# Graph-network layer: SyncE fetches the rows of four whole groups, six a step, where it fetched two groups and the last, four a step

## The reference, cut to what matters

```python
h = jnp.maximum(_layernorm(x, axis=-1), 0.0)
p1 = jnp.tanh(h @ pp_W1 + pp_b1) @ pp_W2 + pp_b2
inter = jnp.concatenate([p1[src], p1[dst]], axis=-1)
inter = (inter @ pi_W1 + pi_b1) @ pi_W2 + pi_b2
inter = (inter @ pi_W3).reshape(E, 64, 8)
i1 = jnp.einsum('ecb,eb->ec', inter, edge_attr)
i1 = jnp.tanh(i1 @ ii_W1 + ii_b1) @ ii_W2 + ii_b2
return x + jax.ops.segment_sum(i1, dst, num_segments=6250)
```

## Time and profile before

| | |
|---|---|
| Median of 3 runs | 1979.13 us (1978.99 to 1981.69) |
| The profiled execution | 1983.09 us, its span 1981.2 us |
| TensorE busy | 1733.1 us (87%) |
| VectorE busy | 1449.0 us (73%) |
| ScalarE busy | 1109.5 us (56%) |
| POOL busy | 1479.1 us (75%) |
| Mean granted TensorE clock | 0.96 of full speed |

### The profile page before, as it was taken

One profiled execution on the slowest core, in us unless ns is written; L12 is line 12 of the kernel. 1 busy time (PEld: TensorE's weight loads), 2 busy tenths in 40 slices (PEclk: granted clock), 3 DMA queues, 4 the chain that ended last, 5 costly groups with the idle time before them and its releaser, 6 DMA issues.

```text
span 1981.2 us, 58993 instructions
## 1 busy us (share of the span) xinstructions
PE 1733.1 (87%) x20012; PEld 1134.5 (57%) x20012; DVE 1449.0 (73%) x1939; ACT 1109.5 (56%) x2419; POOL 1479.1 (75%) x1569
## 2 busy tenths in 40 slices
PE   7699999989988898888888888888888888888998
PEld 6466566655555555555555555555555555555666
DVE  7688778877677777677777777677777767777766
ACT  5666656655555555555555555555555555555554
POOL 7777777777777777777777777777777777777773
PEclk9799999999899999999999999899999999999999
DMA  6543333333333332332333323333233233332331
GB/s 141 115 82 62 67 67 64 61 65 66 58 63 58 62 66 56 63 62 56 62 55 61 62 56 60 61 63 64 55 63 62 56 59 62 59 59 54 59 71 44
DMA packets 266170, 127.83 MB, mean 65 GB/s; under 512 B 188169, under 2 KB 238328, under 8 KB 265864
## 3 DMA queue, kind: packets, MB, share of 16 engines
q1 hardware_dynamic: 214767, 74.86, 17.9%
q0 software_dynamic: 49664, 50.96, 15.4%
q10 hardware_dynamic: 1558, 0.15, 0.1%
HBM read 119.42 MB, written 6.00 MB: 63 GB/s over the span
## 4 chain that ended last, share of the span: by engine, by line
POOL 62%; issue 21%; PE 11%; ACT 2%; DMA 1%; SPq 1%; DVE 1%; ACTq 0%; DVEq 0%; POOLq 0%
POOL u_rows L568 62%; PE bank L1379 5%; PE bank L1474 1%; PE bank L1362 1%; DMA loc_bc<-loc_tab 1%; PE bank L1386 1%; PE spread_ps L1371 1%; DVE o_sb L987 1%; PE bank L1346 1%; ACT st_sb L756 0%; SPq L472 0%; SPq L440 0%; PE spread_ps L1208 0%; PE bank L1356 0%; DMA v_tab<-acc_all 0%
## 5 line engine op out<-in xcount | busy, mean ns | idle before, releaser
L568 POOL DMA_INDIRECT u_rows<-u_tab,src_e x1424 | 1352.4, 950 | 434.1 <-issue 433.1
L987 DVE TENSOR_TENSOR o_sb<-st_sb,spread_ps 128x2048 f32<-128x2048 f32 x391 | 892.9, 2284 | 365.0 <-PE spread_ps L1371 346.8
L756 ACT ACTIVATE st_sb<-bank,s_bias 64x256 f32<-64x256 f32 x1564 | 734.3, 469 | 438.0 <-PE bank L1362 406.9
L1379 PE MATMUL bank<-o_sb,g_sb 128*64 128x256 f32 x6256 | 807.0, 403 | 1.0 <-DVE o_sb L987 0.8
L1379 PEld LDWEIGHTS bank<-o_sb,g_sb 128*64 128x64 f32 x6256 | 433.5, 143 | 232.9 <-issue 36.7
L1362 PE MATMUL bank<-ident,u_rows 128*128 128x128 f32 x1436 | 259.3, 304 | 191.9 <-DMA u_rows<-u_tab,src_e 191.0
L1051 DVE TENSOR_TENSOR hot_t<-loc_bc,bank 126x512 bf16<-126x512 bf16 x391 | 268.8, 688 | 144.0 <-PE bank L1474 59.7
L1362 PEld LDWEIGHTS bank<-ident,u_rows 128*128 128x128 f32 x1436 | 189.8, 192 | 240.5 <-DMA u_rows<-u_tab,src_e 228.0
L1474 PEld LDWEIGHTS bank<-hot,t_sb 128*65 128x65 f32 x3128 | 216.1, 139 | 158.6 <-issue 150.6
L744 ACT ACTIVATE tt_sb<-bank,z_bias 128x256 f32<-128x256 f32 x391 | 185.4, 474 | 175.1 <-PE bank L1379 174.4
L1474 PE MATMUL bank<-hot,t_sb 128*65 128x42 f32 x3128 | 262.8, 235 | 9.1 <-DVE acc_all L1100 8.6
(11 more groups left out here) (148 smaller groups left out, 353.3 us busy)
## 6 DMA issues: line engine op xcount, KB each, us to landing
loc_bc<-loc_tab SPq DMA_DIRECT2D x391, 126.0 KB
u_rows<-u_tab,src_e POOLq DMA_INDIRECT x1424
sp_stage<-u_tab SPq DMA_DIRECT2D x1344, 0.2 KB
v_win<-v_tab SPq DMA_DIRECT2D x391, 15.8 KB
basis<-edge_attr SPq DMA_DIRECT2D x24, 256.0 KB, 4.2
v_tab<-acc_all SPq DMA_DIRECT2D x6, 336.0 KB
basis<-u_tab,src_e POOLq DMA_INDIRECT x100, 2.7
u_tab<-basis SPq DMA_DIRECT2D x6, 224.0 KB
```

The source lines that it names most:

```text
L568: pool.indirect_dma_start(out=u_rows[:, g % UR, j, :] if g >= AHEAD else first_u[:, g - XG, j, :], out_offset=None, in_=u_tab[:, :], in_of ...
L756: last = nc.scalar.activation(tiles[h * D:(h + 1) * D, j], s_ps[part].rearrange("p (q a e) -> p q a e", q=2, a=TILES), ACT.Identity, bias= ...
L987: return nc.vector.tensor_tensor(o_sb[:, r, :, :].rearrange("p c (j e) -> p j c e", j=TILES), st_sb[:, r, :].rearrange("p (j e) -> p j e", ...
L1379: last = nc.tensor.matmul(z_ps[h * D:(h + 1) * D, 0:2 * P], g_sb[:, c, :], o_sb[:, r, c, 2 * h * P:(2 * h + 2) * P], start=(c == 0), stop= ...
```

## The change

SP fetches four whole groups, 96, 183, 270 and 357, and no longer the last one. A fetch takes `ROWS = 6` rows a step, so 86 steps (the last with 2 rows): steps 4 to 89, 91 to 176, 178 to 263 and 265 to 350, 344 fetching steps and 2048 rows. The row numbers lie in one partition of `sp_idx` and are loaded `AT_ONCE = 8` at a time whenever the row's number is a multiple of eight, so three steps of four have one load and the fourth has none: 64 loads a group, 256 in all. The staged group goes to `u_rows` in one DMA of 1 KB a partition in the place of four of 256 bytes. POOL gathers 380 groups where it gathered 381, with group 390 last, for which it also waits for the last input load. The passes of TensorE that stand written out move with the skipped groups.

```diff
-    BY_SP = [(135, 4, P), (263, 132, P), (NG - 1, 260, PART)]
+    ROWS = 6
+    BY_SP = [(96, 4), (183, 91), (270, 178), (357, 265)]
+    AT_ONCE = 8
...
-        sp_idx = sb("sp_idx", [P, len(BY_SP) * TILES], i32)
+        sp_idx = sb("sp_idx", [1, len(BY_SP) * GE], i32)
...
             def load_sp_idx():
-                for k, (g, _, n) in enumerate(BY_SP):
-                    sp.dma_start(sp_idx[0:n, k * TILES:(k + 1) * TILES],
-                                 src[g * GE:g * GE + n * TILES].rearrange("(p j) -> p j", j=TILES)
+                for k, (g, _) in enumerate(BY_SP):
+                    sp.dma_start(sp_idx[0:1, k * GE:(k + 1) * GE], row(src[g * GE:(g + 1) * GE])
                                  ).then_inc(sp_idx_in, 16)
 
-            def fetch_rows(k, p):
-
-                _, at = nc.values_load_multi_w_load_instructions(
-                    sp_idx[p:p + 1, k * TILES:(k + 1) * TILES], engines=[mybir.EngineType.SP], min_val=0, max_val=N - 1,
-                    skip_runtime_bounds_check_because="src names nodes of x")
-                for j in range(TILES):
-                    sp.dma_start(sp_stage[p:p + 1, k % 2, j, :], u_tab[bass.ds(at[j], 1), :]
+            def fetch_rows(k, rows, at):
+
+                for r in rows:
+                    p, j = divmod(r, TILES)
+                    if r % AT_ONCE == 0:
+                        _, at = nc.values_load_multi_w_load_instructions(
+                            sp_idx[0:1, k * GE + r:k * GE + r + AT_ONCE], engines=[mybir.EngineType.SP], min_val=0,
+                            max_val=N - 1, skip_runtime_bounds_check_because="src names nodes of x")
+                    sp.dma_start(sp_stage[p:p + 1, k % 2, j, :], u_tab[bass.ds(at[r % AT_ONCE], 1), :]
                                  ).then_inc(sp_rows_in[k], 16)
+                return at
 
             def place_fetched(k):
 
-                g, _, n = BY_SP[k]
-                sp.wait_ge(sp_rows_in[k], 16 * TILES * n)
-                for j in range(TILES):
-                    sp.dma_start(u_rows[:, g % UR, j, :], sp_stage[:, k % 2, j, :]).then_inc(fetched[k], 16)
+                g, _ = BY_SP[k]
+                sp.wait_ge(sp_rows_in[k], 16 * GE)
+                sp.dma_start(u_rows[:, g % UR, :, :], sp_stage[:, k % 2, :, :]).then_inc(fetched[k], 16)
...
-                    for k, (of, first_at, n) in enumerate(BY_SP):
+                    for k, (of, first_at) in enumerate(BY_SP):
                         if k >= 2 and g == first_at:
                             sp.wait_ge(s_ready, BY_SP[k - 2][0] + 1)
-                        if 0 <= g - first_at < n:
-                            fetch_rows(k, g - first_at)
+                        if first_at <= g:
+                            at = fetch_rows(k, range(ROWS * (g - first_at), min(ROWS * (g - first_at + 1), GE)), at)
...
                 for g in range(XG, NG):
                     k = g // PIECE
+                    if g == FULL:
+                        pool.wait_ge(last_in, 32)
...
-                for of in skipped[:-1]:
+                for of in [of for of in skipped if of < LOOP_END]:
```

More of the change, by code:

```diff
@@ L469, in _ @@
                 load_sp_idx()
+                at = None
                 for g in range(NG):
@@ L560, in _ @@
                     k = g // PIECE
+                    if g == FULL:
+                        pool.wait_ge(last_in, 32)
                     if g % PIECE == 0:
                         pool.wait_ge(ld[k % LD], ld_count(k))
-                    if g in [of for of, _, _ in BY_SP]:
+                    if g in [of for of, _ in BY_SP]:
                         continue
@@ L1409, in y_late @@
                     last.then_inc(y_ps, 1)
-            skipped = [of for of, _, _ in BY_SP]
+            skipped = [of for of, _ in BY_SP]
             def step(n, u, first, last_pass, g=None, fetched_pass=False, gone=(0,) * UN):
@@ L1436, in newest @@
                         if fetched_pass and n + u in skipped:
-                            pe.wait_ge(fetched[skipped.index(n + u)], 16 * TILES)
+                            pe.wait_ge(fetched[skipped.index(n + u)], 16)
                         else:
@@ L1504, in _ @@
                     at += UN
-                with pe.Fori(at, LOOP_END, UN) as n:
-                    for u in range(UN):
-                        step(n, u, False, False, gone=gone)
+                if at < LOOP_END:
+                    with pe.Fori(at, LOOP_END, UN) as n:
+                        for u in range(UN):
+                            step(n, u, False, False, gone=gone)
                 for n in range(LOOP_END, NG + 5, UN):
@@ L1510, in _ @@
                         step(n, u, False, True, fetched_pass=True, gone=gone)
+                        if n + u in skipped:
+                            gone[u] += 1
                 pe.wait_ge(acc_done, NG)
```

## The result

The changed kernel takes 2028.6 us (median of 4, 2026.52 to 2029.3) where the kernel before took 1980.41 beside it: ratio 1.0241, 95% interval 1.0223 to 1.0259. It is 2.4% slower, some 48 us. The side was forecast, the size was not: 1987 us was forecast, with 2000 as the upper end.

What follows compares the result with a forecast made beforehand. SP was taken to bound up to step 350 (1449.7 + 264.6 - 76.5 + 1.8 = 1639.6 us for 330 steps), then TensorE; +8 us on the median 1979.13 gave 1987 us, range 1968 to 2000.

Steps and rivals of the forecast that it cites:

- who would bind: Up to step 350 SP, at 4.97 us a step, sets the pace instead of POOL; from there TensorE does.
- the two ends: Before and behind SP's 330 steps: `loc_bc` of step 20 at 154.6 us; from step 350 at 1794.2 to span end 1988.4.
- the price of a row: On SP, steps 20 to 349: 630 more row fetches at 0.42 us each, +264.6 us.
- rows get dearer in bursts of six: Rival, sharing 10% with TensorE losing clock: row fetches cost more six in a row, giving 2000 us or more.
- Loads: SP's register loads, steps 20 to 349: 244 instead of 330, 86 fewer at 0.89 us, -76.5 us.
- I take the same price for both: SP's register load of eight numbers costs the same as one of four, 0.89 us with its gap.
- The sign named for it: In the profile after, SP's `loc_bc` of step 84 at about 473 us, its step 4.97 us from there to 350.
- the 7.2 of the forecast's sum: Whole span: 1988.4 us forecast against 1981.2 in the profile before, +7.2 us, made +8 for work at step 352.
- the range: 1968 to 2000 us for the whole kernel; the forecast case's own range, SP as the bound, was 1983 to 1998.
- a rule: Rival at 1%: SP's load is priced by the register, some 200 ns each, +0.8 us x 256, about 2190 us.
- POOL's wait: POOL, held by its ring, waits some 10 us in all, most of it before 250 us, in place of 0.9.

Runs made afterwards that it cites:

- The trim of SP's register instructions: The changed kernel without the runtime bounds checks on the window starts: 1983.54 us, ratio 1.0015 to the kernel before the change.

## Why the prediction was wrong

**Right: who would bind.** "Nothing hides this. SP's slack was used to catch up": POOL's share of the chain went from 62% to nothing, TensorE no longer waits for gathered rows, VectorE waits for `loc_bc` until step 350. The trim of SP's register instructions shows it: 45 of the 48 us came back with nothing else changed.

**Right: the two ends.** `loc_bc` of step 20 was forecast at 154.6 and came at 153.87. From `loc_bc` of step 350 to the end of the span 1988.4 - 1794.2 = 194.2 us were forecast and 2026.3 - 1830.43 = 195.9 measured; TensorE did run at 4.45 us a step there with L1400 (L1394 before).

**Right: the price of a row.** 0.42 us was taken for a further row; that is what the records average, in bursts of six too. The rival "rows get dearer in bursts of six" gave the nearest time, 2000 or more, and names the wrong cause: its time came out by luck.

**Wrong: the term "Loads", -76.5 us.** It is the step "I take the same price for both". The rows it rested on, 783 ns for eight window starts and 814 for four row numbers, differ in two things: the window starts are loaded behind row fetches (42 of the 49 loads), the row numbers behind `v_win` (312 of 336). The one costs four numbers more, the other the place, 0.23 and 0.25 us, and they cancelled in the comparison. In place of -76.5 the traces show, for steps 20 to 349: 80 loads behind `v_win` at 1.08, 4 behind an input load at 0.81 and 160 between rows at 0.83, so 223 us, against 330 at the 0.845 that a load took in the saturated stretch before, 279 us: -56. To it comes the second half of the same mistake: 243 steps now have no load ahead of their first row, which takes 0.54 where 0.47 was paid behind a load before: +16. The sum is about -40 and not -76.5, and 36 us is what SP's step was off: (5.08 - 4.97) x 330 = 36.3. The sign named for it, `loc_bc` of step 84 at about 473, came at 479.8. In the spans, 2026.3 - 1981.2 = 45.1 us are these 36, the 7.2 of the forecast's sum and 1.7 behind step 350. The other 3 of the 48 are the place of the two profiled executions among their runs: the one before took 2.7 us more than its median, the one after 0.5 less.

**Wrong: the range.** I wrote that 0.01 us on a row is 19.5 us, and bounded the row. The load I let go only down to 0.81, which bounds it on the side of the rows that I had already compared wrongly. Had each of the 244 loads been given 0.2 us more as an upper end, 49 us, the range would have reached 2036. On the strength of that comparison I had put it down that eight numbers cost no more than four; they cost 0.057 us a number (medians of 560, 787 and 1238 ns for four, eight and sixteen). On it I had also put a rule aside: the Trainium skill, Runtime: NRT & Kernel Launch (Instruction fetch mechanics), gives a TENSOR_LOAD as some 200 ns a register. That page of the Trainium skill speaks of register loads from HBM. For these loads from SBUF the direction holds, and the size, 0.057 us, doesn't.

**Wrong: POOL's wait.** Some 10 us were forecast and 70.7 measured, since a pace of 5.08 falls behind POOL's 4.96 (with the skips) for good. It cost nothing in this kernel, where SP was the bound: the last gather starts at 2001.1 us, its rows land within some 4 us, and TensorE places them at 2010.91.

## What to carry to other kernels

When work moves from the engine that is the bound to one with slack, find the stretch in which the receiving engine is saturated and take its pace from there: 0.63 us of slack a step was all that SP had, and 0.11 us of mispricing a step made 36 us in 330 steps. An instruction's price taken from another line is only good if the instruction ahead of it is the same; compare records in the same place, or bound by the difference. And an engine that will be the bound does not get back what it is held early (10 us in the run without the bounds checks), so new work for its supplier belongs behind the phase in which that one catches up.

## What the runs showed of the hardware

- A register load from SBUF on SP takes 560 ns for four numbers, 787 for eight and 1238 for sixteen (medians), so about 0.33 us and 0.057 a number; 512 loads of four made the kernel 118 us slower than 256 loads of eight.
- Directly behind the issue of `v_win` (126 short pieces, 0.75 us itself) a load takes 0.25 us more than between rows, be it of four, eight or sixteen numbers (medians 807, 1034 and 1486 ns against 557, 778 and 1232), and a row fetch 0.09 more (0.51 against 0.42). It goes by which DMA stands ahead: behind the input load L358 a load of eight takes 0.74 us, no more than between rows, but a row fetch 0.96. Why is open; no run changed `v_win` itself.
- A pair of bounds-check instructions takes 0.265 us on SP from one to the next, and eight such pairs in every eighth step decided between 2.4% and 0.15% slower.
